# A four-block network in one kernel: in its second and fourth attention, the work for the next unit but one is issued three to five steps later within a unit

## The reference

```python
# second attention (L1_ATTN in the kernel): 16 heads of 8 features, not causal
qkv = x @ Wqkv.T + bqkv
out = softmax(q @ k.T / sqrt(8)) @ v
y = out @ Wout.T + bout
# fourth attention (L3_ATTN): latent projections, one key and value head, causal
latent = x @ Wc_down
q, kv = latent @ Wq_up, latent @ Wkv_up
att = softmax(causal(q @ k.T / sqrt(8)))
y = (att @ v) @ Wc_proj
```

## Time and profile before

| What | Value |
|---|---|
| median of 3 runs | 1512.23 us (1511.58 to 1513.2) |
| the profiled execution's own time | 1508.2 us |
| span of the profiled execution | 1506.4 us |
| PE matmul busy | 1193.8 us (79%) |
| DVE busy | 1064.8 us (71%) |
| ACT busy | 724.5 us (48%) |
| POOL busy | 411.6 us (27%) |
| second attention | about 428 to 635 us of the span |
| fourth attention | about 1148 to 1350 us of the span |

### The profile page before, as it was taken

One profiled execution on the slowest core, in us unless ns is written; L12 is line 12 of the kernel. 1 busy time (PEld: TensorE's weight loads), 2 busy tenths in 40 slices (PEclk: granted clock), 3 DMA queues, 4 the chain that ended last, 5 costly groups with the idle time before them and its releaser, 6 DMA issues.

```text
span 1506.4 us, 26816 instructions
## 1 busy us (share of the span) xinstructions
PE 1193.8 (79%) x9110; PEld 837.2 (56%) x9110; DVE 1064.8 (71%) x2986; ACT 724.5 (48%) x1182; POOL 411.6 (27%) x628
## 2 busy tenths in 40 slices
PE   5999989999958777666777874777786999977887
PEld 4666658888823333355344442666674344436776
DVE  7878766666666777445878995688864666647886
ACT  5454523333416767453666782343331466643452
POOL 4545421000023342012454542122311233100110
PEclk8999999999957999878798996799996899997999
DMA  8000000000000000000000000000000000000000
GB/s 325 1 1 1 1 1 1 0 0 0 0 1 1 2 0 1 1 1 1 1 2 0 1 2 1 1 1 1 1 1 1 1 2 0 2 1 1 1 1 29
DMA packets 5845, 14.55 MB, mean 10 GB/s; under 512 B 240, under 2 KB 4464, under 8 KB 5360
## 3 DMA queue, kind: packets, MB, share of 16 engines
q1 hardware_dynamic: 5744, 13.26, 2.3%
HBM read 12.21 MB, written 1.05 MB: 9 GB/s over the span
## 4 chain that ended last, share of the span: by engine, by line
issue 49%; PE 21%; DVE 14%; POOL 6%; ACT 4%; DVEq 4%; POOLq 3%; ACTq 0%
PE PS L1207 3%; PE PS L1155 2%; PE PS L1149 2%; PE PS L1132 2%; POOL trs L412 2%; PE PS L1377 2%; DVE mx L2021 1%; PE PS L1047 1%; POOLq L411 1%; PE PS L1024 1%; POOL hrs L412 1%; DVE w_l0f L2131 1%; DVE sbuf L1923 1%; PE PS L1113 1%; PE PS L1046 1%
## 5 line engine op out<-in xcount | busy, mean ns | idle before, releaser
L2021 DVE TENSOR_REDUCE mx<-PS 128x2 f32<-128x512 f32 (+1 forms) x256 | 155.2, 620 | 81.1 <-PE PS L1155 72.1
L715 ACT ACTIVATE w_l0f<-PS 128x512 f32<-128x512 f32 (+1 forms) x256 | 137.3, 543 | 100.8 <-PE PS L1162 98.1
L410 POOL TENSOR_TENSOR tve<-tmv,eps 128x2 f32<-128x2 f32 x64 | 14.6, 228 | 499.9 <-DVE tmv L1802 331.9
L1752 PE MATMUL PS<-hT_padded,w_l0f 128*128 128x256 f32 x512 | 121.7, 384 | 0.0
L1752 PEld LDWEIGHTS PS<-hT_padded,w_l0f 128*128 128x128 f32 x512 | 94.5, 193 | 10.7
L966 ACT ACTIVATE sg<-PS 128x512 f32<-128x512 f32 x64 | 38.2, 597 | 116.7 <-PE PS L1752 116.6
L410 POOL TENSOR_TENSOR hve<-hmv,eps 128x2 f32<-128x2 f32 x65 | 17.0, 261 | 243.2 <-DVE hmv L1786 108.8
L2950 DVE TENSOR_TENSOR y<-sg,PS 128x512 f32<-128x512 f32 x64 | 44.0, 688 | 49.7 <-ACT sg L966 42.1
L2131 DVE SCALAR_TENSOR_TENSOR w_l0f<-w_l0f 128x768 f32<-128x768 f32 x64 | 67.5, 1054 | 16.4 <-ACT w_l0f L778 15.4
L1529 PEld LDWEIGHTS PS<-w_l2f,y 128*128 128x128 f32 x512 | 71.7, 206 | 13.1 <-ACT y L831 8.7
L1529 PE MATMUL PS<-w_l2f,y 128*128 128x128 f32 x512 | 73.9, 291 | 6.2 <-ACT y L831 5.9
(11 more groups left out here) (478 smaller groups left out, 3282.9 us busy)
## 6 DMA issues: line engine op xcount, KB each, us to landing
w_l0f<-in_l0f SPq DMA_DIRECT2D x1, 3076.0 KB, 17.4
w_l2f<-in_l2f SPq DMA_DIRECT2D x1, 2214.0 KB, 18.8
w_l3f<-in_l3f SPq DMA_DIRECT2D x1, 1736.0 KB, 22.6
w_l0a<-in_l0a SPq DMA_DIRECT2D x1, 960.0 KB, 7.3
result<-X SPq DMA_DIRECT2D x1, 896.0 KB, 4.6
X<-in_x SPq DMA_DIRECT2D x1, 768.0 KB, 10.6
w_l1f<-in_l1f SPq DMA_DIRECT2D x1, 582.0 KB, 14.7
PT<-in_cbf SPq DMA_DIRECT2D x1, 576.0 KB, 8.4
```

The costliest lines, as they stand in the source:

```text
L715: act.activation(P8[:, hh % 8, 0:width], PS[:, hh % 2, 0:width], ACT.Exp, scale=SM_SCALE).then_inc(a["pt"], 1)
L1752: ins = pe.matmul(PS[:, 2 * (c % 2) + g, b * L:(b + 1) * L], w("l0f", "w1")[:, at:at + P], hT[:], start=True, stop=True)
L2021: dve.tensor_reduce(mx[:, hh, 0:nm], PS[:, 2 + hh % 2, 0:nm * keys].rearrange("p (t k) -> p t k", t=nm), AX.X, ALU.max).then_inc(a["mx"], 1)
```

## The change

It moves calls to other steps, on three engines, and moves the waits with them so that bank 7 still passes from user to user. POOL's order stays. No instruction of arithmetic is added or taken away.

| Work | Step before | Step after |
|---|---|---|
| projection, first part (PE) | 0 | 3 |
| projection, second part (PE) | 1 | 4 |
| latent copy, fourth attention (ACT) | 0 | 3 |
| load, second attention (DVE) | 0 and 1 | 3 and 4 |
| load, fourth attention (DVE) | 0 | 4 |
| `head_norm` (DVE) | 4 | 8 |
| first half of keys, second attention (PE, ACT) | 6 | 9 |
| next input: `head_transpose`, `head_copy` | 9 | 10 |
| first half of queries (PE, ACT) | 8 | 12 |

The order of the users of bank 7 is now: second half of the maxima (2), projection (3, 4), first half of the keys (9, second attention alone), the next input (10), first half of the maxima of unit i+1 (11), first half of the queries (12), the rest of the keys (13), second half of the queries (15).

```diff
--- before.py
+++ after.py
@@ -719,8 +719,6 @@
                         A, M, B, D = within(i, 0), within(i, 1), within(i, 2), within(i, -1)
                         lo, hi = slice(0, half), slice(half, 2 * half)
                         for k in range(NH):
-                            if k == 0 and B and l == L3_ATTN:
-                                latent(i + 2)
                             if k < NH - AHEAD and A:
                                 weigh(i, k + AHEAD)
                             if k >= NH - AHEAD and M:
@@ -729,14 +727,16 @@
                                 maxima_copy(i, 1, par)
                             if k == 3 and D:
                                 outputs_copy(i - 1)
-                            if k == 6 and B and l == L1_ATTN:
+                            if k == 3 and B and l == L3_ATTN:
+                                latent(i + 2)
+                            if k == 9 and B and l == L1_ATTN:
                                 parts_copy(i + 2, 0, KTs[par][:, lo])
-                            if k == 8 and B:
-                                parts_copy(i + 2, ntr - 3, QTs[par][:, lo])
-                            if k == 9 and B:
+                            if k == 10 and B:
                                 head_copy(l, i + (head0[l] + 4))
                             if k == 11 and M:
                                 maxima_copy(i + 1, 0, 1 - par)
+                            if k == 12 and B:
+                                parts_copy(i + 2, ntr - 3, QTs[par][:, lo])
                             if k == 13 and B:
                                 parts_copy(i + 2, ntr - 2, KTs[par][:, 0:1] if l == L3_ATTN else KTs[par][:, hi])
                             if k == 15 and A:
@@ -1242,22 +1242,9 @@
 
                             if k == 0 and D:
                                 outputs_transpose(i - 1)
-                            if k == 0 and B:
-                                pe.wait_ge(hd_hT, i + (head0[l] + 3))
-                                pe.wait_ge(a["kq"], (i + 2) * ntr)
-                                if l == L1_ATTN:
-                                    project(i + 2, 0)
-                                else:
-                                    project_down(i + 2)
-                            if k == 1 and B:
-                                if l == L1_ATTN:
-                                    pe.wait_ge(a["ld"], (i + 2) * LOADS[l] + 1)
-                                    project(i + 2, 1)
-                                else:
-                                    project_up(i + 2)
                             if k == 2 and A:
                                 if B:
-                                    pe.wait_ge(a["ld"], (i + 3) * LOADS[l])
+                                    pe.wait_ge(a["kq"], (i + 2) * ntr)
                                 else:
                                     pe.wait_ge(a["kq"], NB * ntr)
                                     pe.wait_ge(a["mev"], 2 * i + 1)
@@ -1266,26 +1253,34 @@
                                 outputs_back(i - 1)
                             if k == 3 and A:
                                 values(i, 0, par)
+                            if k == 3 and B:
+                                pe.wait_ge(hd_hT, i + (head0[l] + 3))
+                                if A:
+                                    pe.wait_ge(a["mev"], 2 * i + 2)
+                                else:
+                                    pe.wait_ge(a["kq"], (i + 2) * ntr)
+                                if l == L1_ATTN:
+                                    project(i + 2, 0)
+                                else:
+                                    project_down(i + 2)
+                            if k == 4 and B:
+                                if l == L1_ATTN:
+                                    pe.wait_ge(a["ld"], (i + 2) * LOADS[l] + 1)
+                                    project(i + 2, 1)
+                                else:
+                                    project_up(i + 2)
                             if k == 4 and D:
                                 project_out(i - 1)
                             if k == 6 and A:
                                 values(i, 1, par)
-                            if k == 6 and B and l == L1_ATTN:
-                                if A:
-                                    pe.wait_ge(a["mev"], 2 * i + 2)
+                            if k == 9 and B and l == L1_ATTN:
+                                pe.wait_ge(a["ld"], (i + 3) * LOADS[l])
+                                keys_transpose(i + 2, range(0, half))
+                            if k == 10 and B:
+                                if l == L1_ATTN:
+                                    pe.wait_ge(a["kq"], (i + 2) * ntr + 1)
                                 else:
                                     pe.wait_ge(a["ld"], (i + 3) * LOADS[l])
-                                keys_transpose(i + 2, range(0, half))
-                            if k == 8 and B:
-                                if l == L1_ATTN:
-                                    pe.wait_ge(a["kq"], (i + 2) * ntr + 1)
-                                elif A:
-                                    pe.wait_ge(a["mev"], 2 * i + 2)
-                                else:
-                                    pe.wait_ge(a["ld"], (i + 3) * LOADS[l])
-                                queries_transpose(i + 2, range(0, half), par)
-                            if k == 9 and B:
-                                pe.wait_ge(a["kq"], (i + 2) * ntr + (ntr - 2))
                                 head_transpose(l, i + 2)
                             if k == 10 and A:
                                 values(i, 2, par)
@@ -1295,8 +1290,11 @@
                                 else:
                                     pe.wait_ge(a["mev"], 2 * i + 2)
                                 maxima_transpose(i + 1, 0, 1 - par)
+                            if k == 12 and B:
+                                pe.wait_ge(a["mev"], 2 * i + 3)
+                                queries_transpose(i + 2, range(0, half), par)
                             if k == 13 and B:
-                                pe.wait_ge(a["mev"], 2 * i + 3)
+                                pe.wait_ge(a["kq"], (i + 2) * ntr + (ntr - 2))
                                 keys_transpose(i + 2, range(half, 2 * half) if l == L1_ATTN else range(1))
                             if k == 14 and A:
                                 values(i, 3, par)
@@ -2068,15 +2066,15 @@
                                 maximum(i + 1, k)
                             if k == 0 and B:
                                 head_stats(X, nxt)
-                            if k < LOADS[l] and B:
-                                if k == 0:
+                            if 5 - LOADS[l] <= k < 5 and B:
+                                if k == 5 - LOADS[l]:
                                     load_ready(i + 2, par)
-                                load_qkv(i + 2, k, par)
+                                load_qkv(i + 2, k - (5 - LOADS[l]), par)
                             if k == 2 and D_:
                                 normalise(i - 1)
                             if k == 5 and D_:
                                 result_stats(i - 1)
-                            if k == 4 and B:
+                            if k == 8 and B:
                                 head_norm(X, nxt, i + (head0[l] + 4))
                             if k == 7 and M:
                                 maximum_parts(0, 1 - par)
```

## The result

The changed kernel takes 1559.07 us in the median of four runs (1554.57 to 1566.14), the kernel before 1511.9 us on the same chip. The ratio is 1.032, with a 95% interval of 1.0297 to 1.0344: 47 us slower. The prediction had 1536.7 us and a range up to 1552.0. The direction was right, the size was half.

The account below looks back on a forecast made before the run. No engine is full; chains of waits between engines bound a unit. Six calls (13.2 us second attention, 9.3 fourth) plus 2.0 for openings add 24.5 us: 1532.7 us profiled, 1536.7 us as median, range 1517 to 1552.

Parts of the forecast that it names:

- The first half of a unit, counted at nothing: Steps 0 to 8 with projection and load moved: no net effect, between a 0.5 us gain and a 0.6 us loss.
- `head_norm` in step 8: On DVE between two maxima, it delays the next input's transpose: 1.1 us per unit in the second attention, 0.35 in the fourth.
- The queries' turn in step 12: An extra passing of bank 7, 1.80 us, delays the keys: 2.65 us per unit in the second attention, 1.6 in the fourth.
- the sum: Per call 2.2 us in the second attention and 1.55 in the fourth, six calls each, plus 2.0 for openings: 24.5 us.
- POOL's splits, "I cost POOL at nothing": POOL's later splits still meet the keys' turn in step 9 just in time and the queries' in 12 with slack: nothing.
- The clock, "I expect the stretch to stay": Second attention: the half-clock stretch stays in most units, so 2.2 us is taken; if it went, 1.2 instead of 2.65.
- rival 4: Half clock comes in the fourth attention too, up to 1.4 us per call, 8 us more, 1545 us; chance 0.13.
- The opening calls: Call i = -1 meets POOL later: between 0 and 2.5 us, taken as 1.0 us for each attention.

Follow-up runs that it names:

- e2: The kernel before with keys in step 9, next input in 10, queries in 12, `head_norm` in 8; projection and load stay in steps 0 and 1: 1543.37 us, ratio 1.0184.
- e1: The kernel before with only the first half of the queries' turn moved, from step 8 to 12: 1532.83 us, ratio 1.0137.
- e4: The kernel before with `head_norm` alone moved on DVE, from step 4 to step 8: 1525.74 us, ratio 1.0077.
- e6: The changed kernel with POOL's tail root ahead of its split of the queries, and that split held until DVE's first `maximum_parts` is done: 1536.8 us, ratio 1.0132.
- e7: The changed kernel with useless matmuls on PE, 8 after step 9 and 4 after step 12, in calls 1 to 5: 1551.4 us, ratio 1.0218.
- e8: The kernel before with useless matmuls, 6 after step 7 and 4 after step 8, in the second attention alone: 1509.49 us, ratio 0.9961.
- e10: The change in the fourth attention alone, the second as in the kernel before: 1534.84 us, ratio 1.0165.
- e9: The change in the second attention alone, the fourth as in the kernel before: 1535.77 us, ratio 1.0162.
- e11: The changed kernel with POOL's tail root first, the queries' split held until `maximum_parts` is done, and 4 useless matmuls after step 9: 1531.62 us, ratio 1.0148.
- e5: The changed kernel with POOL's root for the tail moved ahead of its split of the queries: 1546.96 us, ratio 1.0184.
- e12: The kernel before with e8's useless matmuls and more of them in the opening calls: 1505.53 us, ratio 0.9962.

## Why the prediction was right and wrong

**The first half of a unit, counted at nothing:** right as a duration. Step 8 came 0.5 us earlier in the second attention and 0.2 us earlier in the fourth (11.8 against 12.0), both inside the bounds given. In the second attention `head_norm` out of the way gives back 0.7 us (e2), and the late load takes 0.2 of it.

**`head_norm` in step 8:** right in the fourth attention, where e2 less e1 gives 0.36 us for the 0.35 predicted (alone, in e4, the move costs 0.8). In the second the 1.1 us look met, since the third `values` comes 1.3 us later (17.3 into the unit instead of 16.0). That is luck: in e2, which has the same move, it comes at 15.8, and in e4 the units are no longer than before. In the changed kernel 0.9 us of it are the longer `maximum_parts` (2.1 us in this attention, 1.2 in e2), and half clock has set in as well.

**The queries' turn in step 12:** right in the fourth attention, where the whole back cost 1.56 us against 1.55 and a passing took 1.74 against 1.80. In the second it was too large. The keys' turn comes 2.33 us later in the changed kernel, near the 2.65 predicted, but that too holds the longer `maximum_parts` and the wait for the root. In e2's unit with one half-clock stretch the keys' turn is no later than before (20.6 into the unit against 20.95) and the unit is 1.2 us longer, where the sum carried 2.2.

**POOL's splits, "I cost POOL at nothing": this step failed.** It asked only whether the turns find their data, which they do: PE waits 0.24 us at the keys' turn. It did not ask what else POOL's lateness touches. First, DVE's `maximum_parts` stands at the same time in the unit, and beside POOL's split its instructions stretch, from 1.5 to 2.8 us in the fourth attention; PE's wait before step 10 grows with it from 1.36 (e2) to 2.70 us. The prediction weighed the very rule for this, from the Trainium skill's "SBUF — State Buffer" (section "SBUF: two separate sides"), that the loser of the shared port waits for the other's whole instruction, and applied it to `head_norm` alone. The trace agrees with the rule: an instruction of 0.23 us took 0.94 and ended 0.09 us after POOL's of 1.10. Second, the tail's root stands behind the splits in POOL's queue, and DVE waits for it for 1.66 us. In e6, which cures both (and in the second attention brings the tail's addition beside the split instead), 22 us (by the medians) to 28 us (by the ratios) come back. From first projection to last output transpose its fourth attention is 207.5 us long, against 222.3 in the changed kernel and 198.0 before: of the 24 us lost there in these profiles, 15 hang on this step. That includes half-clock stretches that no longer came, since the full units there are at full clock. By units at full clock the contention costs 1.3 us per call in the fourth (e7 less e6), of which the late load gives back 0.5.

**The clock, "I expect the stretch to stay" and rival 4's "up to 1.4 us per call" at a chance of 0.13: this term was mis-sized.** In the fourth attention, where there was no half-clock stretch, two adjoining ones (6.8 us) came in most units and cost 2.3 us per unit (26.7 against 24.45). In the second, one stretch per unit became two to four. The wait before step 10 in the fourth was predicted at 1.5 us, which is e2's 1.36, and there no stretch came; with the contention it was 2.7, and they came. So in the fourth attention this error follows from the one on POOL. In the second, e2 has up to four stretches without the late load, so there the clock is an error of its own. That it is the clock and not the waits is shown by e7 in the fourth attention and e8 in the second: more work for PE, less time. The Trainium skill's "TensorE: Matmul & The Clock Gate" (section "HAM oscillation — how this bites in real kernels") has recurring waits throttle the engine anew each time. These runs agree in part: each of the ten full units of the changed kernel has such a stretch, but e10 has two units with waits of 2.70 and 2.50 us before step 10 and none.

**The sum, fourth attention, per full unit:**

| Step | Unit, us | Shown by |
|---|---|---|
| before | 22.04 | trace of before |
| back of the change | 23.60 | e2 |
| with the late load, `maximum_parts` undisturbed | 23.12 | e6 |
| with the late load and its contention | 24.45 | e7; e10's units at full clock |
| with the half-clock stretches | 25.2 to 27.1 | trace of after |

The predicted 23.6 is the second row. In the second attention single units allow a rougher split. At one half-clock stretch each, a unit was 23.7 us before, 24.9 in e2, and 25.9 with the whole change, in the one such unit of e9:

```profile
563.15:589.07 25.92, 18.58 (x197) 9.08 (x197) 18.28 (x49) 16.44 (x26) 8.43 (x13) 0.93 0.00 0
```

So the back costs 1.2 us and the front 1.0, and the further stretches bring the changed kernel to 27.6 to 28.5: about half of the 22 us is clock, an estimate that rests on single units.

**The opening calls, 1.0 us for each attention and a share of the six calls:** wrong in the second. From the first projection to the first full unit it took 60.8 us instead of 62.1; in the fourth 56.6 instead of 53.8, near the 2.55 us of the sum.

What decides in a given unit whether a half-clock stretch comes was not settled: e10 has both kinds side by side.

## What to carry to other kernels

When work moves later in a unit, follow it to the engine that takes it up and write down what runs beside it there and what stands behind it in that engine's queue; that the next user finds its data in time is only one of three questions. Keeping two instructions apart by a wait can push the later one onto the next neighbour, as in e11. A longer wait on PE may have to be priced twice, as time and as clock: in the fourth attention 1.36 us before step 10 cost no clock in ten units, and 2.5 to 2.7 us brought half clock in most, at a price (2.3 us) above that of the wait. Where PE has waits that cannot be removed, a few matmuls of no use inside them can pay: 0.4% here.

## What the runs showed that was not expected

The half-clock stretches vary from execution to execution of the same kernel, and with them the time of layers that nobody touched: the part between the two attentions took 518.1 to 531.8 us in these profiles. The changed kernel's four runs spread over 11.6 us; those of the kernel before spread over 4.2 in the first four and over 18.2 in the thirteen beside e5 to e8. A profile of one execution is therefore a poor measure of the whole, and a good one of a unit whose clock one can see. In e12, raising the clock from 0.60 to 0.74 in a stretch whose pace PE's clock does not set gave nothing at all.
